# Last block of the model: a final pass over four-row runs with four buffers per sum, and row buffers cleared by GpSimd

## The reference, cut to what matters

```
x = x.reshape(-1, 256)                                   # 4096 tokens, layer-normed before
shared = silu(x @ shared_wg.T) * (x @ shared_wu.T) @ shared_wd.T
scores = sigmoid(x @ gate_w.T)                           # 64 experts
topw, topi = top_k(scores, 8);  topw = topw / topw.sum(-1, keepdims=True)
buf[e, pos] = x[token]                                   # per expert, room for 256 rows, the rest dropped
out_buf = silu(buf @ expert_wg) * (buf @ expert_wu) @ expert_wd
routed[token] = sum over its 8 choices of topw * out_buf[e, pos]
x3 + tanh(g_ffn[1]) * (shared + routed)
```

## Time and profile before

| | us |
|---|---|
| median of 3 runs | 2617.09 |
| lowest, highest | 2615.79, 2618.28 |
| the profiled execution, its span | 2623.7 |
| routing block ends, expert block starts | about 2140 |
| first gather on POOL | 2146.21 |
| last adding DMA issued by POOL | 2564.19 |
| final pass, first load issued by SP | 2568.11 |

### The profile page before, as it was taken

One profiled execution on the slowest core, in us unless ns is written; L12 is line 12 of the kernel. 1 busy time (PEld: TensorE's weight loads), 2 busy tenths in 40 slices (PEclk: granted clock), 3 DMA queues, 4 the chain that ended last, 5 costly groups with the idle time before them and its releaser, 6 DMA issues. The chain is left out here.

```text
span 2623.7 us, 54622 instructions
## 1 busy us (share of the span) xinstructions
PE 1866.5 (71%) x22307; PEld 1389.7 (53%) x22308; DVE 1286.0 (49%) x2422; ACT 823.7 (31%) x1484; POOL 561.4 (21%) x519
## 2 busy tenths in 40 slices
PE   4777777776477456898888889788657647667764
PEld 3545554543376334676766667566435525445543
DVE  4444544442677315676666666666447741111113
ACT  2333333322222132433444444234225531111110
POOL 1111111110000110100110210001010027888880
PEclk8888889888688775887887888787866659899895
DMA  4454445442211343223223321411012126556566
GB/s 91 89 99 85 82 94 104 81 85 50 83 58 62 123 90 76 62 51 66 68 64 70 78 66 38 78 28 33 23 57 79 64 72 136 115 129 127 129 115 198
DMA packets 234029, 216.37 MB, mean 82 GB/s; under 512 B 62724, under 2 KB 212718, under 8 KB 233312
## 3 DMA queue, kind: packets, MB, share of 16 engines
q1 hardware_dynamic: 200224, 179.01, 29.0%
q0 software_dynamic: 24576, 27.05, 6.2%
q10 hardware_dynamic: 9024, 7.35, 0.9%
HBM read 147.08 MB, written 72.45 MB: 84 GB/s over the span
## 5 line engine op out<-in xcount | busy, mean ns | idle before, releaser
L1233 DVE TENSOR_TENSOR r_score<-r_ps_s,r_score 128x512 f32<-128x512 f32 x256 | 172.8, 689 | 66.1 <-PE r_ps_s L1483 62.3
L2039 DVE TENSOR_TENSOR e_hT<-e_sil,e_ps_gu 128x256 f32<-128x256 f32 x64 | 26.9, 421 | 324.3 <-ACT e_sil L2061 196.9
L1212 DVE TENSOR_TENSOR r_score<-r_score,r_ps_t 128x1024 f32<-128x1024 f32 x128 | 154.6, 1218 | 47.8 <-PE r_ps_t L1463 45.8
L1323 ACT ACTIVATE r_score<-r_ps_s 128x512 f32<-128x512 f32 x256 | 145.7, 612 | 100.0 <-PE r_ps_s L1452 98.8
L1452 PE MATMUL r_ps_s<-r_q,r_rk 96*128 96x64 bf16 x2048 | 148.7, 236 | 26.8 <-ACT r_score L1323 13.4
L1452 PEld LDWEIGHTS r_ps_s<-r_q,r_rk 96*128 96x128 bf16 x2048 | 128.2, 119 | 55.2 <-ACT r_score L1323 24.7
L2068 ACT ACTIVATE e_y<-e_ps_y,e_rows 128x256 f32<-128x256 f32 x128 | 53.6, 470 | 327.2 <-DMA base_scratch<-e_y,k_token 163.4
L2000 POOL DMA_INDIRECT e_rows<-rows_w_scratch,k_token x128 | 134.9, 1054 | 96.6 <-DVE e_h_last L2027 57.7
L313 DVE TENSOR_REDUCE a_row_max<-a_ps_s 128x2 f32<-128x512 f32 (+1 forms) x192 | 127.4, 685 | 56.9 <-PE a_ps_s L478 51.6
L1483 PE MATMUL r_ps_s<-r_q,r_k 96*128 96x64 bf16 x2048 | 115.7, 203 | 45.7 <-DMA r_k<-parts_scratch 30.9
L1310 ACT ACTIVATE r_score<-r_score 128x1024 f32<-128x1024 f32 x128 | 136.7, 1080 | 24.6 <-DVE r_score L1212 24.0
(11 more groups left out here) (297 smaller groups left out, 4248.8 us busy)
## 6 DMA issues: line engine op xcount, KB each, us to landing
a_q<-parts_scratch SPq DMA_DIRECT2D x96, 128.0 KB, 4.1
a_k<-parts_scratch SPq DMA_DIRECT2D x96, 128.0 KB, 4.2
r_q<-parts_scratch SPq DMA_DIRECT2D x96, 128.0 KB, 3.1
e_wg<-in_L_ffn_expert_wg SPq DMA_DIRECT2D x64, 128.0 KB
e_wu<-in_L_ffn_expert_wu SPq DMA_DIRECT2D x64, 128.0 KB
e_wd<-in_L_ffn_expert_wd SPq DMA_DIRECT2D x64, 128.0 KB
r_k<-parts_scratch SPq DMA_DIRECT2D x4, 1536.0 KB, 14.3
rows_w_scratch<-m_row SPq DMA_DIRECT2D x8, 640.0 KB, 3.2
```

The source lines that it names most:

```text
L1212: dve.tensor_tensor(part, part, bcast(ps_t[m % 2][:], NT), ALU.add).then_inc(shifted, 1)
L1233: dve.tensor_tensor(part, ps_s[c % 2][:].rearrange("p (c e q) -> p c q e", c=4, e=2), part, ALU.add).then_inc(added, 1)
L1323: act.activation(by_query[1 - par][:, c // 8, :, q0:q0 + 8, :], ps_s[c % 2][:].rearrange("p (q c e) -> p c q e", c=HC, e=2), ACT.Copy).the ...
```

## The change

Three things change.

- The seven row buffers get a longer life and are cleared in the routing block, by POOL, behind its last `invert`; POOL waits for its own memsets there. The DVE memsets and the waits of POOL and PE on `blanked` in the expert block go. DVE keeps the two small memsets of `h_last`.
- In the final pass a partition holds four neighbouring tokens: `(r p g)` in place of `(r g p)`. Each partition then reads and writes one run of 4 KB. So that the late choices meet the same tokens, PE takes every fourth column of `late_T` as its stationary operand.
- The sums have NB = 4 buffers each, and four semaphores for loads and four for writes, in place of two.

```
@@ routing block, POOL
             for r in range(R):
                 if r + 1 < R:
                     invert(r + 1)
+            for u in range(ROWS):
+                pool.memset(rows[u][:], 0.0).then_inc(blanked, 1)
+            pool.wait_ge(blanked, START + ROWS)
@@ expert block, POOL
-            pool.wait_ge(blanked, START + ROWS)
             for e in range(AHEAD):
                 gather(e)
@@ expert block, DVE
-            for u in range(ROWS):
-                dve.memset(rows[u][:], 0.0).then_inc(blanked, 1)
             for b in range(2):
                 dve.memset(h_last[b][:], 0.0).then_inc(blanked, 1)
-            dve.wait_ge(blanked, START + ROWS + 2)
+            dve.wait_ge(blanked, START + 2)
@@ expert block, PE
                 pe.wait_ge(gathered[e % ROWS], 32 * (e // ROWS + 1))
-                if e == 0:
-                    pe.wait_ge(blanked, START + ROWS)
@@ final pass, layout
-        sum_rows = [a.rearrange("(r g p) d -> r p g d", g=G, p=P) for a in sums]
-        out_rows = out.rearrange("b s d -> (b s) d").rearrange("(r g p) d -> r p g d", g=G, p=P)
+        sum_rows = [a.rearrange("(r p g) d -> r p g d", g=G, p=P) for a in sums]
+        out_rows = out.rearrange("b s d -> (b s) d").rearrange("(r p g) d -> r p g d", g=G, p=P)
@@ final pass, SP (DVE and ACT take their buffers r % NB in the same way)
-                if r >= 2:
-                    sp.wait_ge(out_written[r % 2], START + r // 2 * 16)
-                sp.dma_start(sum0[r % 2][:], sum_rows[0][r]).then_inc(sums_loaded[r % 2], 16)
-                sp.dma_start(sum1[r % 2][:], sum_rows[1][r]).then_inc(sums_loaded[r % 2], 16)
+                if r >= NB:
+                    sp.wait_ge(out_written[r % NB], START + r // NB * 16)
+                sp.dma_start(sum0[r % NB][:], sum_rows[0][r]).then_inc(sums_loaded[r % NB], 16)
+                sp.dma_start(sum1[r % NB][:], sum_rows[1][r]).then_inc(sums_loaded[r % NB], 16)
@@ final pass, PE
-                        tile = r * G + 2 * n + t
-                        ins = pe.matmul(late_banks[r % 2][n][:, t * D:(t + 1) * D], late_T[:, tile * P:(tile + 1) * P], y_last[:],
+                        first = r * N + 2 * n + t
+                        ins = pe.matmul(late_banks[r % 2][n][:, t * D:(t + 1) * D], late_T[:, first:(r + 1) * N:G], y_last[:],
                                         start=True, stop=True)
```

More of the change, by code:

```diff
@@ L1572, in expert_ffn @@
     token = keep.enter_context(nc.sbuf_tensor("k_token", [P, E * C], U32))
+    ROWS = 7
+    rows = [keep.enter_context(nc.sbuf_tensor(f"k_rows{i}", [P, C, W], F32)) for i in range(ROWS)]
     with ExitStack() as stack:
@@ L1622, in expert_ffn @@
         high_ready, low_ready, mapped = sem("high_ready"), sem("low_ready"), sem("mapped")
+        blanked = sem("blanked")
         own_ready, tile_ready = sem("own_ready"), sem("tile_ready")
@@ L1945, in expert_ffn @@
         UN = 4
-        ROWS = 7
         AHEAD = ROWS - 1
-        rows = [sb(f"rows{i}", [P, C, W], F32) for i in range(ROWS)]
         wg, wu, wd = ([sb(f"{n}{i}", [P, *shape], F32) for i in range(UN)] for n, shape in
@@ L1953, in expert_ffn @@
         y_last = sb("y_last", [E, D], F32)
-        sum0, sum1 = ([sb(f"{n}{i}", [P, G, D], F32) for i in range(2)] for n in ("sum0_", "sum1_"))
+        NB = 4
+        sum0, sum1 = ([sb(f"{n}{i}", [P, G, D], F32) for i in range(NB)] for n in ("sum0_", "sum1_"))
         ps_turn, ps_gu, ps_y = ([pb(f"{n}{i}", [P, 512], F32) for i in range(2)] for n in ("ps_turn", "ps_gu", "ps_y"))
@@ L1964, in expert_ffn @@
             sem(n) for n in ("last_summed", "last_copied", "late_ready", "planes_added", "total_ready"))
-        sums_loaded, out_written = ([sem(f"{n}{i}") for i in range(2)] for n in ("sums_loaded", "out_written"))
+        sums_loaded, out_written = ([sem(f"{n}{i}") for i in range(NB)] for n in ("sums_loaded", "out_written"))
         block = stack.enter_context(nc.Block())
         up = lambda a: a.rearrange("e (t p) i -> e p t i", p=P) if len(a.shape) == 3 else a.rearrange("(e t p) i -> e p t i", e=E, p=P)
-        sum_rows = [a.rearrange("(r g p) d -> r p g d", g=G, p=P) for a in sums]
-        out_rows = out.rearrange("b s d -> (b s) d").rearrange("(r g p) d -> r p g d", g=G, p=P)
+        sum_rows = [a.rearrange("(r p g) d -> r p g d", g=G, p=P) for a in sums]
+        out_rows = out.rearrange("b s d -> (b s) d").rearrange("(r p g) d -> r p g d", g=G, p=P)
         late_banks = (ps_turn, ps_gu)
@@ L2044, in _ @@
             for r in range(R):
-                dve.wait_ge(sums_loaded[r % 2], START + 32 * (r // 2 + 1))
-                dve.tensor_tensor(sum0[r % 2][:], sum0[r % 2][:], sum1[r % 2][:], ALU.add).then_inc(planes_added, 1)
+                dve.wait_ge(sums_loaded[r % NB], START + 32 * (r // NB + 1))
+                dve.tensor_tensor(sum0[r % NB][:], sum0[r % NB][:], sum1[r % NB][:], ALU.add).then_inc(planes_added, 1)
                 dve.wait_ge(planes_added, START + r + 1)
@@ L2049, in _ @@
                     dve.wait_ge(late_ready, START + 2 * r + n + 1)
-                    part = sum0[r % 2][:, 2 * n:2 * n + 2, :].rearrange("p g d -> p (g d)")
+                    part = sum0[r % NB][:, 2 * n:2 * n + 2, :].rearrange("p g d -> p (g d)")
                     dve.tensor_tensor(part, part, late_banks[r % 2][n][:], ALU.add).then_inc(total_ready, 1)
@@ L2071, in _ @@
                 act.wait_ge(total_ready, START + 2 * r + 2)
-                act.dma_start(out_rows[r], sum0[r % 2][:]).then_inc(out_written[r % 2], 16)
-            for i in range(2):
-                act.wait_ge(out_written[i], START + 16 * R // 2)
+                act.dma_start(out_rows[r], sum0[r % NB][:]).then_inc(out_written[r % NB], 16)
+            for i in range(NB):
+                act.wait_ge(out_written[i], START + 16 * R // NB)
         @block.tensor
```

## The result

| | before | changed |
|---|---|---|
| median, us | 2617.12 | 2604.86 |
| lowest, highest (4 runs each) | 2615.79, 2618.28 | 2593.82, 2606.88 |
| the profiled execution's own time | not given | 2593.82 |
| its span | 2623.7 | 2592.0 |

The ratio is 0.9947, 95% interval 0.9927 to 0.9968: 13.9 us less, between 8.4 and 19.1. The forecast was 20.1 less. The median of 2604.86 lies in the range for 8 in 10 (2591.5 to 2606), but above the forecast's own range (2592 to 2601). A second batch of 12 runs against 23 gave 0.9947 again (0.9931 to 0.9963).

What follows compares the result with a forecast made beforehand. POOL bounds the expert loop, with the seam's memsets on the path, and a load-add-write chain bounds the final pass. Seam -5.0, memsets +1.0, pass -16.1: -20.1, median 2597.0 us; own range 2592 to 2601, 8 in 10 2591.5 to 2606.

Steps and rivals of the forecast that it cites:

- rival A: Final pass: 4 KB runs no faster, only buffers help; pass 45.7 us, gain 9.9, sum -13.9, 2603.2 us; chance 0.12.
- Seam, -5.0: Barrier to POOL's first gather: gather 5.0 us earlier without DVE's memsets, distance to first adding DMA still 20.4 us.
- D: Seam gains nothing because ACT's wait is fixed in time, and memsets cost DVE 4.3: -11.8, 2605.3 us; chance 0.06.
- Memsets beside DVE, +1.0: Routing round 7: four tensor_scalars each wait for one POOL memset, DVE 2.4 us late, 1.0 taken as cost.
- Final pass, -16.1: Final pass bound by bytes at 395 GB/s: 39.5 us against 55.6, gain 16.1, ends 9.9 and 20.0.
- Length of runs: Final pass loads: 9.5 ns cost per packet, so 4 KB runs give 395 GB/s where 1 KB runs give 337.
- Number in flight: Final pass: four rounds requested at once, first write done by about 12 us, DMA engines never dry until last loads.
- Over 380 GB/s: Final pass: sign of the forecast, with DMA share 0.9 or more from 3 us after the first issue on.
- The 2.0 for gaps: Final pass: 2.0 us added for what no chain of full rates has, share being 0.74 where load and write overlap.
- Stride, 0: PE's weight load in the final pass: columns 16 bytes apart cost nothing, up to 140 ns more being free.
- B: Final pass: strided weight load doubles to 667 ns, if clock stays 0.50; pass 44.3, sum -15.3, 2601.8 us; chance 0.12.
- C: Final pass: strided weight load goes up by four to 1333 ns; pass 75.9 us, sum +16.3, 2633.4; chance 0.05.

Runs made afterwards that it cites:

- e3: Kernel before with the new final pass alone (4 KB runs, four buffers), rows still cleared by DVE at the seam: 2601.02 us, ratio 0.9914-0.9955.
- f2: Kernel before with four buffers per sum in the final pass, 1 KB runs kept, rows cleared by DVE: 2604.62 us, ratio 0.9911-0.9949.
- f3: Kernel before with 4 KB runs and strided stationary operand in the final pass, two buffers per sum kept: 2620.90 us, ratio 0.9982-1.0023.
- f1: Changed kernel plus six zero matmuls on PE ahead of its wait for round 7's normalised rows: 2603.73 us, ratio to kernel before 0.9900-0.9946.
- e1: The changed kernel as it is, timed again in 12 runs: 2604.82 us, ratio to the kernel before 0.9931-0.9963.
- f4: Changed kernel with every final-pass load reading the same first four tokens for all partitions, real sums left out: 2605.77 us in one run, no ratio.
- e2: Kernel before with the row memsets alone moved to POOL late in routing, final pass as before: 2617.62 us, ratio 0.9976-1.0014.
- h1: Changed kernel with POOL's memsets early in routing, eight buffers per sum, 1 KB runs, contiguous stationary operand: 2605.55 us, ratio to kernel before 0.9919-0.9966.
- g3: Repeat of the changed kernel with POOL's memsets ahead of routing's first power, four buffers, 4 KB runs: 2596.15 us, ratio to kernel before 0.9888-0.9922.
- e4: Changed kernel with POOL's memsets ahead of its first power of routing instead of behind the last: 2597.02 us, ratio to kernel before 0.9901-0.9948.
- g1: Changed kernel with POOL's memsets early in routing and eight buffers per sum, 4 KB runs: 2601.40 us, ratio to kernel before 0.9913-0.9948.

## Why the prediction was near in sum, and where its steps were off

The measured 13.9 us less is also, to the tenth, rival A's sum. That is a coincidence of terms: A has 9.9 for the pass and 1.0 for the memsets, the profiles 15.1 and 3.7.


**Seam, -5.0: right.** Measured 6.36 to 1.43, -4.9. The distance to the first adding DMA came out at 18.95, not 20.4: ACT's 3.62 us of "remote" idleness were of that one execution. e3, f2 and f3, which keep the seam as it was, have 18.5, so a row met once should not have been made a landmark. D's first half, a gain that turns into a wait, holds in small: against those 18.5 the ten kernels with the early gather lose 0.6 by their mean of 19.1.

**Memsets beside DVE, +1.0: mechanism right as far as it went, size wrong, +3.7.** The seven memsets took 4.07 us (forecast 4.3), and DVE was 2.34 late (forecast 2.4). The way there was another: not one memset per tensor_scalar, but one tensor_scalar behind all that were left. The forecast let 1.4 through to PE and took 1.0; f1's 1.7 agrees. What failed is the step that lets through to PE only DVE's lateness less a slack of 0.95 us ("about 1.4 us would come through") and puts nothing behind it. After PE's new wait the clock was at 0.50 for most of the next eight us, where it is 1.00 otherwise, and that cost about 2.0 more. The prediction priced a wait by its length and forgot what PE does next. The Trainium skill ("SBUF — State Buffer", section Who interferes with whom) describes DVE (in the modes that use both of its port pairs, which a tensor_scalar can enter) and GpSimd excluding one another for whole instructions. The 2761 ns row agrees, but there and in e1, f1 and f4 (2756 to 2773 ns) the exclusion outlasted several instructions of POOL; in e2 it did not.

**Final pass, -16.1: the sum right (-15.5 between the two profiles), its reasons mostly not.**
- Length of runs. The forecast's step from 337 to 395 GB/s, a cost of 9.5 ns per packet, was worth 45.7 - 39.5 = 6.2 us. The 45.7 doesn't come out of the forecast's own terms: 2.2 + 37.3 + 1.2 + 2.2 + 2.0 = 44.9, so the step was 5.4 and A's gain 10.7. Measured 1.4 with four buffers. The row behind "337 at full share" was no ceiling: f2 moves 345 GB/s of the same 1 KB runs and h1 368, at shares of 1.05 and 1.09. A share of 0.97 with two buffers had not meant that the engines could do no more.
- Number in flight. It is worth 13.8, where rival A gave it 9.9. A said the runs don't matter: nearly right, with the wrong price (45.7, or 44.9, against 41.5).
- Transfer. Over 380 GB/s were named as the sign; it was 360. Loads alone do reach the forecast's 395: from 3 to 8 us after the first load, with the first write issued only at 7.5, e1, e3, f1 and g3 move 392 to 414 GB/s, though the changed kernel and e4 move 351 and 344. The forecast carried the rate of loads alone through loads and writes together. 12.58 MB at 360 are 34.9 us, not 31.9. The 2.0 for gaps were counted on top of a rate that was too high; without it, 2.2 + 34.9 + 1.2 + 2.2 = 40.5 against 40.1. Two errors cancelled. The ninth load went out 15.2 us after the first, not by 12: writes that share the engines with loads take 5.6 us to land, not 3.8.
- The limit of 358 GB/s per core that the prediction weighed seemed to fit the 360 of four buffers. g1 measures 389 over 18 us of mixed loads and writes, so it is not the bound here. The Trainium skill's "HBM Reference", section Specifications (TRN2), says as much: 358 is the share when both cores of a pair stream, and one alone gets more. No run here has the second core streaming.

**Stride, 0: right.** 329 ns against 333, DVE never waits for PE, PE's round is 3.6 to 3.8 us. B and C are out. The doubling on DVE that B was built on compares a reduction with a tensor_scalar, so it never showed that the stride was the cause. The remark that the clock might rise in the pass was wrong: 0.50 throughout.

**Sum.** -4.9 + 3.7 - 15.1 (the pass by means) = -16.3, or -15.7 with the 0.6 behind the seam; both lie inside the measured -8.4 to -19.1. The forecast's -20.1 lies outside it. It is 3.8 lower than -16.3, of which 2.7 are the memsets and 1.0 the pass.

## What to carry to other kernels

In a pass of loads, a little arithmetic and writes, count how many transfers are requested before the first wait: going from two to four buffers gave ten times what longer runs gave, and going on to eight still gave 2.5 us in one profile. When work is moved to an idle engine, ask which instruction of its neighbour it then stands beside; a place with nothing beside it (here the start of routing) gives the gain without the loss. Price a new wait on PE by what PE does afterwards, not by its length.

## What the runs showed of the hardware

- POOL memsets of 128x640 f32 (0.58 us each), which read nothing, stopped a DVE tensor_scalar of 128x256 f32 for 2.76 us, until all seven were done; so in four of five profiles. In the fifth (e2) the longest took 0.79 us and the seven memsets 4.63 in place of 4.07.
- A wait of 0.46 to 1.56 us on PE, ahead of the turn of the last round, goes with a granted clock of 0.50 through the next matmuls in all four kernels that have it: sixteen take 3.27 to 3.65 us, 1.97 in the others. Zero matmuls in its place (f1) brought them back to 1.97.
- The DMA share goes over 1 (1.09 in h1) and rate still rises: 327 GB/s at 0.97 before, 368 at 1.09, same run length. A share near 1 is no proof of a full engine.
- A stationary operand of fp32 columns 16 bytes apart loads in 329 ns, a contiguous one in 333, both at a granted clock of 0.50.
- Loads that read one 4 KB source for all 128 partitions are slower than loads from 128 sources: 312 against 360 GB/s over 30 us of the pass, in one run.
